# Cross-attention and a routed FFN on one core: images taken in pairs, transposed scores in row tiles

## The reference, cut to what matters

```python
# x: 64 images x 128 tokens x 128, ctx_768: 64 x 77 x 96; 16 heads of width 8
def xattn(x, cond, q_w, q_b, kv_w, kv_b, proj_w, proj_b):
    q = (x @ q_w + q_b).reshape(B, N, 16, 8).transpose(0, 2, 1, 3)
    kv = (cond @ kv_w + kv_b).reshape(B, 77, 2, 16, 8)
    k, v = kv[:, :, 0].transpose(0, 2, 1, 3), kv[:, :, 1].transpose(0, 2, 1, 3)
    attn = softmax(einsum('bhnd,bhmd->bhnm', q * 8 ** -0.5, k), axis=-1)
    out = einsum('bhnm,bhmd->bhnd', attn, v).transpose(0, 2, 1, 3).reshape(B, N, 128)
    return out @ proj_w + proj_b
# ffn: layer norm, router of 8 experts, top 2, hidden width 512, silu
x = x + xattn(layernorm(x), ctx_768, ...)
x = x + ffn(layernorm(x), gamma, beta, router_w, W1, W2)
```

## Time and profile before

| | us |
|---|---|
| median of 3 executions | 844.96 |
| profiled execution, its own time | 845.43 |
| span of the profile (first to last instruction) | 843.5 |
| TensorE busy | 721.3 |
| VectorE busy | 543.0 |
| ScalarE busy | 499.3 |
| GpSimd busy | 492.0 |

### The profile page before, as it was taken

How to read it: one execution, slowest core, us unless ns; L and a number is a source line. 1 busy time by engine, 2 the same in 40 slices (tenths; PEclk the granted TensorE clock), 3 DMA queues, 4 the chain that set the end, 5 groups by cost and what they waited for, 6 DMA issues and landing times. The chain is left out here.

```text
span 843.5 us, 16697 instructions
## 1 busy us (share of the span) xinstructions
PE 721.3 (86%) x5164; PEld 496.7 (59%) x5164; DVE 543.0 (64%) x1857; ACT 499.3 (59%) x1037; POOL 492.0 (58%) x692
## 2 busy tenths in 40 slices
PE   1699999998989899998999977988899889999960
PEld 1455556555656555564665545766677677777840
DVE  1456666765776667675666734666677777688972
ACT  1366666565566566564666544856675766677840
POOL 5422526657566747665765560664577777765772
PEclk9699989988999989998999965989999999999995
DMA  5455454554565537455442434655987875779964
GB/s 180 110 115 135 113 135 115 161 122 130 118 159 145 139 81 186 101 158 121 105 105 67 100 107 167 202 192 192 318 301 241 290 214 185 254 246 366 377 214 179
DMA packets 152287, 146.49 MB, mean 174 GB/s; under 512 B 53403, under 2 KB 108584, under 8 KB 152040
## 3 DMA queue, kind: packets, MB, share of 16 engines
q1 hardware_dynamic: 140808, 121.57, 50.0%
q0 software_dynamic: 9088, 19.68, 6.8%
q10 hardware_dynamic: 2304, 4.20, 1.3%
HBM read 81.56 MB, written 40.86 MB: 145 GB/s over the span
## 5 line engine op out<-in xcount | busy, mean ns | idle before, releaser
L837 ACT ACTIVATE P<-pt 77x512 f32<-77x512 f32 x256 | 151.5, 593 | 117.3 <-PE pt L641 108.8
L1350 POOL DMA_INDIRECT ys<-yo,to x156 | 167.6, 1074 | 75.2 <-issue 39.6
L1343 POOL DMA_INDIRECT xs<-zz,idx x128 | 131.1, 1024 | 94.8 <-PE pt L563 35.3
L973 DVE TENSOR_REDUCE mx<-ps 128x4 f32<-128x308 f32 x256 | 118.8, 471 | 88.4 <-PE ps L628 84.3
L1213 DVE TENSOR_TENSOR sl<-sf,sh 128x512 fp32r<-128x512 f32 x156 | 107.2, 691 | 63.6 <-ACT sh L884 28.3
L641 PE MATMUL pt<-qd,kc 128*77 128x512 f32 x256 | 115.2, 451 | 15.6 <-DMA qd<-nm 14.9
L652 PE MATMUL po<-P,v 77*9 77x128 f32 x2048 | 107.2, 284 | 4.8 <-ACT osb L845 4.5
L628 PE MATMUL ps<-kd,qc 128*128 128x308 f32 x256 | 107.5, 421 | 1.6 <-DMA kd<-kc 0.9
L882 ACT ACTIVATE sf<-ps 128x512 f32<-128x512 f32 x78 | 46.9, 601 | 68.8 <-PE ps L563 46.6
L641 PEld LDWEIGHTS pt<-qd,kc 128*77 128x77 f32 x256 | 38.9, 152 | 50.5 <-issue 29.1
L628 PEld LDWEIGHTS ps<-kd,qc 128*128 128x128 f32 x256 | 50.6, 198 | 25.9 <-issue 19.9
(11 more groups left out here) (207 smaller groups left out, 1802.7 us busy)
## 6 DMA issues: line engine op xcount, KB each, us to landing
qd<-qc SPq DMA_DIRECT2D x128, 128.0 KB
ws<-wsd SPq DMA_DIRECT2D x26, 512.0 KB
w1o<-wsd SPq DMA_DIRECT2D x26, 512.0 KB
w2o<-wsd SPq DMA_DIRECT2D x26, 512.0 KB
xb<-xs SPq DMA_DIRECT2D x39, 288.0 KB
kd<-kc SPq DMA_DIRECT2D x128, 77.0 KB
wsd<-ws SPq DMA_DIRECT2D x8, 1024.0 KB
y<-ys SPq DMA_DIRECT2D x32, 256.0 KB
```

Source lines behind the costliest of these rows:

```text
L837: eng.activation(P[k % 4][:, :], pT[k % 2][0:CS, :], ACT.Exp, scale=SCALE).then_inc(sems["p"], 1)
L973: eng.tensor_reduce(mx[b % 2][:, 4 * g:4 * g + 4], ps[k % 2][:, 0:KC].rearrange("p (j m) -> p j m", j=4), AX.X, ALU.max, negate=True).then ...
L1343: eng.indirect_dma_start(out=xs, out_offset=at, in_=zz[b][:, j % 4, :], in_offset=None).then_inc(sems[f"sw{b}"], 16)
L1350: eng.indirect_dma_start(out=ys, out_offset=at, in_=yo[u % NYO][:, q, :], in_offset=None).then_inc(sems[f"ys{u % NYO}"], 16)
```

## The change

The unit is now a pair of images p (32 of them). A slot of the list is one pair; two written-out patterns, one for even and one for odd slots, hold the steps of the pair and of the projections. LATER and SOONER say how many slots a step of a pair, or quads a step of a quad, stands from the slot.

```diff
-K1 = 18
+K1 = 16
-SLOTS = "SC0 Pv2 ST0 ON SC1 Pv3 ST1 MT SC2 ST2 PR Pu0 OT SC3 ST3 Pu1"
+EVEN = ("ST00 CT XT EX00 ST01 SC10 EX01 SC11 KP PV SC12 KL SC13 MT QP OE ND QL ON A0 "
+        "ST10 EX10 ST11 SC00 KG0 EX11 SC01 KG1 OT SC02 KG2 SC03 KG3 PR A1 A2 LX")
+ODD = ("KD0 ST00 EX00 ST01 SC10 QG0 EX01 SC11 QG1 PV SC12 QG2 SC13 MT QG3 OE ND ON XH VP "
+       "ST10 EX10 ST11 SC00 KD1 EX11 SC01 OT SC02 XP SC03 PR")
+LATER = {"ST": 1, "EX": 1, "PV": 2, "OE": 2, "OT": 2, "ON": 3, "PR": 3, "MT": 0, "ND": 0, "SC1": 0, "SC0": -1}
...
-COUNTED = (7, 11, 12, 15)
-BANKED = ("XT", "QP", ...
+COUNTED = (7, 10, 11, 15)
+BANKED = ("SC", "XT", "QP", ...
...
-        xin = tile(sa, "xin", [128, 4, 128], F, 4)
+        xin = tile(sa, "xin", [128, 4, 128], F, NX)          # NX = 6
-        qd = tile(sa, "qd", [128, 2, 4, 4, S], R, 2)
-        v9 = tile(sa, "v9", [CS, 4 * H, 9], F, 2)
-        P = tile(sa, "P", [CS, 4 * S], F, 4)
+        v18 = tile(sa, "v18", [CS, 2, 2, H, 18], F, 2)
+        P = tile(sa, "P", [CS, 4, 4, S], F, 4)
-        pm, ps, pT, po = pt("pm", 3), pt("ps", 2), pt("pt", 2), pt("po", 1)[0]
+        pm, po = pt("pm", 3), pt("po", 1)[0]
+        pT = st.enter_context(nc.psum_tensor("pt", [128, 4, 512], F))
...
-            def QD(p):            # SyncE: four DMAs qd <- qc for two images
-            def MT(b):            # SyncE: one DMA qd <- nm for an image
...
+            def SC(p, i, g):      # TensorE: as before, but into a bank of pm
+                t, s, n = bank("SC", p, i, g)
+                w.wait_ge(s, n)
...
+            def MT(p):            # one transpose of 32 maxima for the pair
+                eng.transpose(t[0:32, 0:128], mx[p % 2][:, :], idf[:, :]).then_inc(sems["mT"], 1)
+
+            def ST(p, i, h):
+                c, n_ = p // 2, 2 * (p % 2) + i
+                w.wait_ge(f"nm{p % 2}", 64 * (p // 2 + 1))
+                w.wait_ge("p", 4 * p + 2 * i + h - 1)
+                for g in range(4):
+                    for j in (2 * h, 2 * h + 1):
+                        at_j = slice(32 * j, 32 * j + 32)
+                        ins = eng.matmul(pT[0:CS, j, g * S:(g + 1) * S], kc[c % 2][at_j, n_, g, :], qc[c % 2][at_j, n_, g, :],
+                                         start=True, stop=True)
+                ins.then_inc(sems["T"], 1)
+
+            def PV(p):
+                w.wait_ge("p", 4 * p + 4)
+                w.wait_ge("osb", p)
+                for g in range(4):
+                    for i in range(2):
+                        for j in range(4):
+                            ins = eng.matmul(po[32 * j:32 * j + 18, g * 128:(g + 1) * 128], v18[c % 2][:, p % 2, i, 4 * g + j, :],
+                                             P[(2 * p + i) % 4][:, j, g, :], start=(i == 0), stop=(i == 1))
+                ins.then_inc(sems["Og"], 1)
...
+            def ND(p):            # ScalarE: four DMAs nm -> row 32j+24 of qc itself
+                for j in range(4):
+                    eng.dma_start(qc[c % 2][32 * j + 24:32 * j + 25, i:i + 2, :, :].rearrange("p i g n -> p (i g) n").bitcast(F),
+                                  nm[p % 2][8 * j:8 * j + 8, :].bitcast(F)).then_inc(sems[f"nm{p % 2}"], 16)
+
+            def EX(p, i, h):      # ScalarE: two banks of pt at once, 77x1024
+                two = slice(2 * h, 2 * h + 2)
+                eng.activation(P[(2 * p + i) % 4][:, two, :, :], pT[0:CS, two, :].rearrange("m j (g n) -> m j g n", g=4), ACT.Exp,
+                               scale=SCALE).then_inc(sems["p"], 1)
```

More of the change, by code:

```diff
@@ L63, in stage_order, with slot @@
     at = lambda c, *names: [(n, c) for n in names] if 0 <= c < NC else []
[L64 to L76, removed]
+    gap = lambda n: [None] * int(n)
+    def slot(s):
+        k, odd = divmod(s, 2)
+        steps = []
+        for name in (ODD if odd else EVEN).split():
+            stem, digits = name.rstrip("0123456789"), [int(d) for d in name if d.isdigit()]
+            if stem == "A":
+                steps += at(k + 2, name)
+            elif stem == "KD":
+                steps += [("KD", 2 * k + 2 + digits[0])] if 0 <= k + 1 < NC else [None]
+            elif stem in SOONER:
+                c = k + SOONER[stem]
+                steps += [(stem, c, *digits)] if 0 <= c < NC else [None]
+            else:
+                p = s - LATER[name[:3] if stem == "SC" else stem]
+                steps += [(stem, p, *digits)] if 0 <= p < NP else []
+        return steps
     def norms(c):
@@ L117, in go, with routed @@
             put(steps.pop(0) if steps else None)
[L119 to L133, removed]
[L134 to L153 removed]
+    def routed(c):
+        turned = tails[0].index(("ZT", c)) if ("ZT", c) in tails[0] else -4
+        tails[1].extend(gap(max(turned + 4 - len(tails[1]), 0)) + router(c))
+    ok = lambda p: 0 <= p < NP
+    for s in range(-6, NP + 4):
+        k, odd = divmod(s, 2)
+        if odd and 0 <= k - 2 < NC - 1:
+            tails[0] += norms(k - 2)
+        if odd and 0 <= k - 3 < NC - 2:
+            routed(k - 3)
+        if s >= 2 and s % 3 == 2 and s // 3 < E:
+            put(("WL", s // 3))
+        if s >= 4 and s % 3 in (1, 2) and (s - 4) // 3 < E:
+            put(("WS", (s - 4) // 3, s % 3 - 1))
+        for step in slot(s):
+            put(step)
+            go()
+    routed(NC - 2)
     tails[0] += norms(NC - 1)
[L155 removed]
+    routed(NC - 1)
     blocks = True
@@ L381, in xattn_moe @@
         flat = lambda t: t[:, :, :].rearrange("p a b -> p (a b)")
-        hid = ps + pT
+        hid = [pT[:, k, :] for k in range(4)]
         W2v = W2.rearrange("e (k p) d -> e p k d", p=128)
@@ L673, in PR @@
+            def PR(p):
+                w.wait_ge(*freed("ON", p))
+                t, s, n = bank("PR", p)
                 w.wait_ge(s, n)
-                eng.matmul(t[:, 0:128], oT[b % 2][:, :], pwf[:, :], start=True, stop=True).then_inc(sems["pr"], 1)
+                for i in range(2):
+                    ins = eng.matmul(t[:, i * 128:(i + 1) * 128], oT[p % 2][:, i, :], pwf[:, :], start=True, stop=True)
+                ins.then_inc(sems["pr"], 1)
             def ZT(c):
@@ L853, in ZT, with ON @@
+            def ON(p):
+                t, s, _ = bank("ON", p)
+                w.wait_ge("onT", p + 1)
+                w.wait_ge("pr", p - 1)
+                eng.copy(oT[p % 2][:, :, :], t[:, 0:256].rearrange("p (i d) -> p i d", i=2)).then_inc(sems[s], 1)
             def ZT(c):
```

268 lines of the change are left out of this document (104 added, 164 removed).

## The result

The changed kernel takes 1023.65 us (median of 4 runs, 1015.66 to 1037.02) against 844.38 for the kernel before beside it (4 runs, 840.59 to 849.12): a ratio of 1.209, interval 1.199 to 1.219. The ratio is taken from the runs in the faster of two states, without the 1037.02, and so isn't the quotient of the two medians. The prediction was 802 us, its range 755 to 858. So it had the wrong sign, and none of its rivals names what happened.

A forecast was written before the change was run, and what follows sets the result against it. TensorE's queue was taken as the attention stage's bound. PV -2.8, OT and MT -1.1, ST +2.0, the stall -1.1 make -3.0 us a quad, -45 over 15 quads; +2 at the edges: 802 us from 845.4, range 755 to 858.

The forecast's parts named there:

- PV: PV's visits on TensorE fall from 16 to 2 a quad, streaming unchanged: -2.8 us a quad.
- the 0.20 of a switch: Each PV visit on TensorE costs 0.08 us to enter and 0.12 to leave, on top of its streaming.
- OT and MT: Output transposes fall from 16 to 8, transposes of maxima from 4 to 2, on TensorE: -1.1 us a quad.
- ST, the unknown: Row-tiled ST on TensorE: weight loads in turn, 0.53 plus 0.20 a visit, eight visits 5.8 us, +2.0 a quad.
- the first rival: ST's row tiles overlap in full: 0.44 us a visit, 3.5 a quad, 768 us in all; chance 0.23.
- the sentence on the stall: ST's wait for the maxima's DMA goes, and with it the clock's fall: -1.1 us a quad.
- clock 1.00 in nearly all: Sign in the attention stage: quads of 26 us instead of 29.0, nearly all at granted clock 1.00.
- Both stay hidden: ScalarE (17.7 to 20.0 of 26 us a quad) and VectorE (at most 18.9) stay hidden under TensorE.
- Banks: SC joins the ring of three shared banks, 40 uses a quad instead of 32: 0 taken, up to +6 kept.
- the ring's mark: Sign of the ring as bound: TensorE's waits for VectorE sum to above 20 us in the attention stage.
- the rival's 6.0: The ring of shared banks becomes the bound: 0.15 us a use, 6.0 a quad, 892 us in all; chance 0.11.
- Edges: Filling and emptying the pipeline of pairs some 10 us longer, TensorE having less to do but not nothing: +2 us.

The follow-up runs named there:

- 7: The kernel before with PV's four visits an image made as one: 825.6 us, before 806.5.
- 12: The kernel before with the maxima's DMA issued by ScalarE, then with one PV visit an image on top: 845.3 us, ratio 1.006 to before.
- 2: The changed kernel with ST on all 128 rows, same number of products and columns: 901.8 us, before 808.0.
- 8: The changed kernel with the ST of before (block-diagonal q, two 512-column products a visit): 889.1 us, before 803.0.
- 3: The changed kernel with each SC product computed twice more, 32 added products a quad: 928.3 us, before 808.0.
- 9: The kernel of 8 with the maxima's DMAs (ND) issued by SyncE instead of ScalarE: 837.9 us, before 803.0; again 837.9, before 809.2.
- 1: The changed kernel with the four DMAs of the maxima (ND) issued by SyncE instead of ScalarE: 949.9 us, before 808.0.
- 6: The changed kernel with SC on two banks of its own, ST's halves sharing two instead of four: 1028.7 us, before 806.5.
- 12's first: The kernel before with the maxima's DMA issued by ScalarE instead of SyncE: 797.3 us, before 803.0; again 832.7, before 841.3, ratio 0.989.
- changed, repeat: The changed kernel itself, nothing altered, run again in a later batch: 1005.3 us, before 806.5.
- 11: The changed kernel with ND on SyncE and each SC product computed twice more: 895.3 us, before 841.3, ratio 1.064.

## Why the prediction was wrong

By its steps, with the prices in us a quad where it had them so:

- *PV: right.* 1.87 us a visit, 1.9 predicted, and by 7 the 0.20 of a switch is saved. But TensorE's saved time became idle time and a lower clock; over the whole kernel it gave nothing (12).
- *OT and MT: right in count;* nothing speaks against 0.11 an instruction, no run tried it alone.
- *ST, the unknown: the wrong one of the two prices, on the safe side.* A visit costs 0.42, not 0.73; two behind each other 0.45. So the loads of 77 columns don't queue, fp32r with 128 columns goes at the rate of 512, and the tiles stream together. Since three quarters of the visits stand in such pairs, ST costs 2.2 us a quad, where the sum had 5.8 and the first rival 3.5. The same products on all rows go at 1.17/16 = 0.073 us each (2), near the 0.066 that the text took for a load, but also near the 0.06 of its streaming, so whether the loads set the pace there isn't shown. A visit alone is near the first rival's price of 0.44. The rule of the Trainium skill (TensorE: Matmul & The Clock Gate, part 3), which stood beside that rival, is borne out by this trace: four tiles cost 0.03 us more than two. It says nothing of what the clock then does, and by it alone the kernel should have taken 768 us.
- *The step that failed* is the sentence on the stall: "So the wait should be gone, and with it the clock's fall", and with it "clock 1.00 in nearly all" quads. The first half is right, the wait fell from 14.1 us to 3.0. The second half took for granted that the clock falls only behind a stall. In the changed kernel it is low for hundreds of microseconds in which TensorE is busy 85 to 90%, and the longest wait of TensorE for another engine, 60 to 480 us, is 2.3 us. Putting ST back on whole-array products (8) gave back 116 us and the clock rose from 0.58 to 0.89; feeding all rows in the same products (2), 103 and 0.87; adding whole-array products beside the row tiles (3), 77 and 0.87.
- *What decides the clock, and what stays open.* That ST's row tiles are the main cause is shown by 8, which takes them out and leaves the pairs. What the three have in common is that more of the array streams for more of the time. Before, ST streamed all 128 rows for 3.8 us a quad; changed, each product streams 32 of them for 0.06 us, and the 64 products come to what 0.96 us on all rows would be, a quarter. In 2 and 8 the rows fed and the time streamed grow together, and the changes of tiling around ST go, so which of these the clock answers to isn't told apart; only that the changes of tiling alone don't hold it down is seen in 3, which keeps them at 0.87. The Trainium skill (TensorE: Matmul & The Clock Gate, Part 1) tells the clock by how busy TensorE has been lately. By that rule the changed kernel's 85% should earn a higher clock than the 77% of 8; the rows show the reverse, so if the rule is to hold, busy has to mean something narrower than the busy time of a profile. Nor is it told apart whether something else of the pair structure also lowers it a little: 8 has 0.89, and the 0.95 of before came back only with ND moved (9).
- *"Both stay hidden": wrong for both.* First ScalarE. An issue of the maxima's DMA takes 0.627 us, the upper of the two rows used. The sum was right, 5.0 us a quad, and the text named what stands behind it, "ON's copy and the next exponential"; it then set the cost to 0 since ScalarE's total of 20 us fits in a quad of 26. But an engine's total says nothing about the place: the copy that waits frees a bank of the ring for TensorE. Measured are 3.5 us a quad (8 to 9) and 3.1 (1), of the 5.0 given as the most, and much of it comes by the clock. Then VectorE, whose total fitted too: MT behind SC13 waits for its last reduction, 21.7 us in 420, a term that the sum doesn't have.
- *Banks: 0 taken, up to 6 kept; a small part measured.* The text set a sum of TensorE's waits for VectorE above 20 us as the ring's mark. The sum is 42.5 in the changed kernel, but the mark can't tell the ring: its largest part, 21.7, is MT's wait for its operand and stays at 22.4 with the scores out of the ring (6). What a bank held by a reduction costs in the kernel of 9 is 0.6 us a quad of TensorE's waits, a tenth of the rival's 6.0; banks held by other results, the router's and oT's, come on top.
- *Edges: +2 taken, +12 measured* in the changed kernel: +25 at the start, -13 at the end. The prediction reckoned with 10 us of filling and took TensorE's work in it as nearly full cover.

**The account**, in the batches where before takes 803 to 809. From 1005 us, ST's effect on the clock takes 116 (8), ND 51 (9). That leaves 838, at the clock of before. The means over the 15 quads, cut at the output transposes, with the clock between the first and the last cut:

| | quad | TensorE busy | idle | clock |
|---|---|---|---|---|
| before (the 845 us profile) | 29.0 | 26.7 | 2.2 | 0.96 |
| before, nm issued by ScalarE (12's first) | 27.5 | 26.0 | 1.5 | 0.98 |
| changed, repeat | 39.9 | 33.9 | 6.0 | 0.58 |
| 1, ND on SyncE | 36.8 | 31.2 | 5.6 | 0.64 |
| 8, block ST | 32.8 | 25.7 | 7.1 | 0.87 |
| 9, block ST and ND on SyncE | 29.25 | 23.8 | 5.5 | 0.95 |

Against the kernel of before with most of its stall gone (12's first, 797.3, same batch as 8 and 9) 41 us stand: 23 at the start (first output transposes at 72.8 us instead of 49.4), 26 in the quads (29.25 instead of 27.54), and 8 given back at the end. The 26 are 34 us less of TensorE's busy time and 59 more in which it doesn't work.

Where did the saved work of PV, OT and MT go, the 3.9 us a quad? Most of it was saved: in the kernel of 9 TensorE is busy 23.8 us a quad, where before it was 26.7. But the quad isn't shorter. The time that TensorE doesn't work grew from 2.2 to 5.5 us. By the list of its waits 2.2 of the 5.5 is MT's wait for the pair's last reduction (32.0 us in 420), where the largest wait for another engine was 4.6 us in 420 before. The rest is in small waits: 8.8 in 420 for a result of the router, 8.6 for other reductions, 6.9 for the DMA of the maxima, 6.5 and 6.2 for the router's counts and the copies of kc, and smaller ones. TensorE had been the bound by so little that 3 us less of it met the next one, the hand-overs between engines: of operands, as for MT, and of the three shared banks.

## What to carry to other kernels

Before packing small products into tiles of the array, ask what else keeps it streaming: a change that makes TensorE's stream shorter by using fewer rows can cost the clock, and then everything on TensorE costs up to twice as much, so predict the granted clock of the stage and not only the count of products. And a step that reads a reduction's result wants other work ahead of it in TensorE's queue: a reduction that is hidden by its engine's total isn't hidden from the step right behind it. An engine's share of busy time is no cover for a DMA issue: look at what is queued behind the issue and whose bank it frees. Before a longer unit of the pipeline, price its filling as a term of its own.

## What the runs showed that wasn't expected

- The granted clock doesn't go by TensorE's busy share in the stage. In order of the share: before 92%, 0.95; changed with PV split 90%, 0.55; changed 85%, 0.58; ND on SyncE 84%, 0.64; added products 81%, 0.87; block ST with ND on SyncE 81%, 0.95; full rows 79%, 0.87; block ST 77%, 0.89; SC with its own banks 76%, 0.65. All versions below 0.7 have ST in row tiles; of those above, only the two with the added products (3 and 11) have.
- Adding 32 products a quad whose results are thrown away made the kernel 77 us faster.
- Eight fp32r products of 128 columns in two row tiles, with 77 columns of weights each, take 0.42 us with the change of tiling and sixteen in four row tiles 0.45: the loads too go side by side.
- A DMA issue on ScalarE that moves 8 rows of nm into one partition took 627 ns, where one of the output's took 338; for that time nothing queued behind it on ScalarE started.
- Batches of runs differ by 5%: the kernel before took 803 us in one and 844 in another. That it is the chip isn't shown, since the record gives the number 3 both to a batch at 808 and to the one at 841. The difference lies mostly behind the attention stage: of the 36 us between the two profiles of 12's first kernel (span 794.9 and 830.5) 24 come after the last quad.
